# Row sums of a banded softmax: one reduction on VectorE in place of eight accumulators on ScalarE, with the units of all engines in a new order

## The reference

```python
def local_attention(q, k, v):
    b, h, n, d = q.shape
    w = n // WINDOW
    bq = q.reshape(b, h, w, WINDOW, d) * QK_SCALE
    ...
    sim = jnp.einsum('bhwid,bhwjd->bhwij', bq, bk)
    ...
    mask = (i < j) | (i > j + WINDOW) | (j == -1)
    sim = jnp.where(mask, -jnp.finfo(sim.dtype).max, sim)
    attn = jax.nn.softmax(sim, axis=-1)
    out = jnp.einsum('bhwij,bhwjd->bhwid', attn, bv)
```

## Time and profile before

| | |
|---|---|
| median of 3 runs | 1740.66 us (1738.55 to 1747.6) |
| profiled execution | 1741.72 us, its span 1739.9 us |
| granted TensorE clock, mean | 0.924 of full speed |
| PE busy | 1434.9 us, 82% |
| VectorE (DVE) busy | 1254.2 us, 72%, 2201 instructions |
| ScalarE (ACT) busy | 1268.0 us, 73%, 2878 instructions |
| GpSimd (POOL) busy | 367.3 us, 21% |

### The profile page before, as it was taken

How to read it: one execution, slowest core, us unless ns; L and a number is a source line. 1 busy time by engine, 2 the same in 40 slices (tenths; PEclk the granted TensorE clock), 3 DMA queues, 4 the chain that set the end, 5 groups by cost and what they waited for, 6 DMA issues and landing times.

```text
span 1739.9 us, 32913 instructions
## 1 busy us (share of the span) xinstructions
PE 1434.9 (82%) x13044; PEld 849.7 (49%) x13044; DVE 1254.2 (72%) x2201; ACT 1268.0 (73%) x2878; POOL 367.3 (21%) x222
## 2 busy tenths in 40 slices
PE   3667697889888998888889887789798898988986
PEld 1122454345556554445456534555345564656664
DVE  6999978565886549968786878764977685477554
ACT  5523792779668787787798484878588985898875
POOL 2000000003144130410252021221003451045440
PEclk8776996899999999899999998989899998999998
DMA  7774224013023012323003433003320140000100
GB/s 250 232 242 138 73 76 98 3 26 74 11 52 60 23 39 84 117 81 121 19 19 81 92 105 103 16 9 88 106 98 17 24 94 10 10 17 20 31 20 19
DMA packets 70985, 121.75 MB, mean 70 GB/s; under 512 B 6864, under 2 KB 28112, under 8 KB 69072
## 3 DMA queue, kind: packets, MB, share of 16 engines
q1 hardware_dynamic: 70832, 119.65, 24.5%
HBM read 89.34 MB, written 15.60 MB: 60 GB/s over the span
## 4 chain that ended last, share of the span: by engine, by line
PE 36%; ACT 28%; DVE 28%; issue 5%; DMA 1%; POOL 0%; SPq 0%; ACTq 0%; DVEq 0%; POOLq 0%
ACT tiles L1591 8%; ACT L1425 5%; PE psum L602 5%; DVE neg_max L1197 5%; DVE tiles L1119 5%; PE psum L848 4%; DVE tiles L1113 2%; DVE tiles L1123 2%; PE psum L880 2%; ACT tiles L1535 2%; ACT tiles L1632 2%; PE psum L881 2%; PE psum L833 2%; PE psum L980 2%; PE psum L947 2%
## 5 line engine op out<-in xcount | busy, mean ns | idle before, releaser
L1754 POOL TENSOR_TENSOR tiles<-tiles 128x1024 f32<-128x1024 f32 x64 | 155.1, 2424 | 669.7 <-DVE tiles L1376 669.7
L602 PE MATMUL psum<-cst,tiles 128*128 128x128 f32 x1408 | 211.4, 287 | 87.9 <-DVE tiles L1337 32.6
L602 PEld LDWEIGHTS psum<-cst,tiles 128*128 128x128 f32 x1408 | 163.3, 146 | 164.9 <-issue 102.5
L1591 ACT ACTIVATE tiles<-psum,lmax,invn 128x128 f32<-128x128 f32 x512 | 226.3, 470 | 15.2 <-DVE lmax L1247 11.8
L1197 DVE TENSOR_REDUCE neg_max<-psum 128x2 f32<-128x1024 f32 (+3 forms) x176 | 189.8, 1117 | 32.5 <-PE psum L800 32.3
L673 PE MATMUL psum<-tiles,cst 128*128 128x512 f32 x256 | 152.4, 728 | 43.1 <-DVE tiles L1123 43.1
L1765 POOL TENSOR_TENSOR tiles<-tiles,lsum 128x1024 f32<-128x1024 f32 x64 | 126.9, 1983 | 280.7 <-DVE lsum L1251 280.7
L1425 ACT ACT_TABLE_LOAD x124 | 159.1, 1283 | 2.9 <-PEq L1968 0.7
L1119 DVE TENSOR_TENSOR_SCAN tiles<-tiles 128x512 f32<-128x512 f32 x128 | 157.2, 1259 | 2.7 <-ACT tiles L1484 0.5
L1484 ACT ACTIVATE tiles<-tiles,colp 128x512 f32<-128x512 f32 x128 | 90.3, 719 | 87.3 <-DVE tiles L1119 79.1
L1232 DVE TENSOR_REDUCE ssq<-tiles 128x16 f32<-128x1024 f32 x64 | 77.8, 1215 | 86.3 <-ACT tiles L1680 86.0
(11 more groups left out here) (226 smaller groups left out, 3324.4 us busy)
## 6 DMA issues: line engine op xcount, KB each, us to landing
tiles<-bc_scratch SPq DMA_DIRECT2D x128, 512.0 KB, 4.8
v_prev<-tiles SPq DMA_DIRECT2D x112, 128.0 KB, 2.3
split_scratch<-tiles SPq DMA_DIRECT2D x96, 128.0 KB, 2.4
tiles<-split_scratch SPq DMA_DIRECT2D x32, 384.0 KB
wts<-in_wts SPq DMA_DIRECT2D x1, 3114.0 KB, 15.8
tiles<-in_x SPq DMA_DIRECT2D x8, 256.0 KB, 3.8
out<-tiles SPq DMA_DIRECT2D x8, 256.0 KB, 2.7
tiles<-in_rowp SPq DMA_DIRECT2D x1, 768.0 KB, 7.4
```

What stands on the lines that cost most here:

```text
L602: ins = nc.tensor.transpose(ps[:, j * 128:(j + 1) * 128], src[:, j * 128:(j + 1) * 128], ident)
L1591: ins = fn(pr[:, i * 128:(i + 1) * 128], ps[:, i * 128:(i + 1) * 128], ACT.Exp, bias=own(lmax)[:, b, i:i + 1], scale=own(invn)[:, j, 0, 2 ...
L1754: tt(T(TURNED, 2), T(TURNED, 2), T(TURNED + 2, 2), ALU.add).then_inc(sem("qk_sum"), 1)
```

## The change

Three edits. l_exp no longer accumulates. l_inv first reduces the 128x1024 probabilities in SBUF to eight sums, waits for its own reduction, and takes the reciprocal. ORDER and BANKS are replaced as a whole, for all engines; network(), the units and their number stay (1570 units on PE, 1226 on VectorE, 1394 on ScalarE, 202 on GpSimd, 204 on SyncE), and the order now gives 125 table loads where it gave 124.

```diff
 def l_inv(l, j):
     dve.wait_ge(*at("l_exp", l, j))
+    step(nc.vector.tensor_reduce(own(lsum)[:, j % 2, :], T(LP, 2).rearrange("p (i n) -> p i n", n=128), AX.X, ALU.add))
+    settle()
     nc.vector.reciprocal(own(lsum)[:, j % 2, :], own(lsum)[:, j % 2, :]).then_inc(sem("l_inv"), 1)
...
             ins = fn(pr[:, i * 128:(i + 1) * 128], ps[:, i * 128:(i + 1) * 128], ACT.Exp,
-                     bias=own(lmax)[:, b, i:i + 1], scale=own(invn)[:, j, 0, 2 * g + e:2 * g + e + 1],
-                     accum_out=own(lsum)[:, b, i:i + 1])
+                     bias=own(lmax)[:, b, i:i + 1], scale=own(invn)[:, j, 0, 2 * g + e:2 * g + e + 1])
...
 ORDER = {
     "PE": (
...
-        "65745f65865b65c65d65e65965a65f"),
+        "55e75855f75b75c75975a75d75e75f"),
...
 BANKS = (
...
-    "65432502456704676574570656746204654545432043257270717257041040650431240135243767567675767657657657")
+    "02140767276535675657430274645606756724570454564230103743737603450765076767760760667607107176076010")
```

More of the change, by code:

```diff
@@ L312 @@
[L312 to L318 removed]
+        "80010000010110200100210300380130030130210420030310520120200420300510610700600730430510820410900800920530630710a20610c10b"
@@ new lines @@
+        "00a10f10e10d00c10g00b00f00e00d20710h00g10i30810j00h00i30900j10k20810l10n10p10m10o10q30a10r00k00l00n00p00m00o00q30c00r10s"
+        "30b10t10u10v10w20920a30f30e30d20c00s30g00t00u00v00w20b30h10y10x10z11011111211b11g11e11c11d11i11f11h11711911811411511311a"
+        "11600y00x00z01101001230i01b20f01g01e20e01d01c11j01f20d01i01h01711l11k11n01411m11o11q11p11s11r11w11t11v01830j11x11z12111u"
+        "11y12312012212412612712512901901a12812a12c12e12b12d12f12h12i12g12k01512j12l12n12p30k12m12o01312q01620g12r30l12s30n12t30p"
@@ new lines @@
+        "01j30m30o30q20h30r01l01k01n20i01m01o01q01s01p01r01w01v12u01t20j12v01x01z02101u01y12w02002202302613502402702502902802a02c"
+        "12x02e12y02b02d13402f02h02i30s02g02k02j02l02n30t02m02o02p12z13613702q13d02r30v02s30u30w02t13013120k13813213f13e13g13320l"
+        "13m20n20p13a13913h20m20o20q13b13n13o20r13p13c13j13i13q13k02u13l02v02w03513s13r30y30x13t13u30z13v02x31002y20s13w03402z20t"
+        "13x20v20u20w31114214313y13z14014103603714403003114503d14614714g03803203e03331214814914f14a03f03g03m03a03903h31b03b14h03n"
@@ new lines @@
+    "POOL": (
+        "80180010000010110230010410510310710810610a10b10910c00100220000400500310d10e00700800610g10h10f00a00b00910j10k10i00c10m10n"
+        "10l10o00d00e00g00h00f00j00k00i00m00n00l00o30130230430530330730830620120230a30b30920420520330c20720820650020a20b20920c30d"
+        "30e30g30h30f30j30k20d30i20e30m30n40020g20h30l20f20j30o20k20i20m20n20l20o401700402600501502404405403504505503407408406506"
+        "50750840a40b60160250a40950b50960460560360760860660a60b60960c40c50c60d60e60g60h60f70170260j60k60i60m60n70460l70570340d40e"
+        "60o70770870640g40h70a70b70970c50d50e40f40j40k50g50h40i40m40n50f50j50k40l50i50m50n40o70d70e50l70g70h70f50o70j70k70i70m70n"
+        "70l70o"),
@@ new lines @@
+    "SP": (
+        "10000080480180680780880080280580380980a20080b101001300102103002003104301105201004005302303106202107006007203304305108204"
+        "10900800920530630720620730830920820910a10b10c00a00b00c10d10e00d00e10f10g30a10h30b10i30c00f00g20a20b20c10j00h10k00i10l10m"
+        "00j00k10n50000l50150200m30d30e50350450550650750850900n40040140220d20e40330f40430g40540640740840930h20f20g30i20h50a50b20i"
+        "50c30j30k20j20k30l40a30m40b40c20l20m30n70040d40e70170270370470570660020n70770850d60170950e60260360460560660760860940f40g"
+        "50f50g70a60a60b70b60c70c60d60e40h40i50h60f60g70d50i70e60h60i60j60k70f70g60l60m70h70i60n40j50j40k50k40l70j40m70k50l50m70l"
+        "70m40n50n70n"),
@@ L329 @@
[L329 to L332 removed]
+    "012101020000101212122340454510440440001104514411041041041415210024202104206420606060604620420420640235635057075305305702"
@@ new lines @@
+    "020467026400274062035032507024602476737654320203573046046702357373573203042600462343642040160304505125732374134735430714"
+    "071761767107603507074201750232430735425432012302562201673621025632525670574347347067264701037037124012612045473052747041"
+    "021010102463452061430670670602460246767027474626076476076276742066230401035701351312354560264060240260126012402352426045"
+    "020254046760245057607607013570724624062013503753576030303013535315771103103405703707765065346350107106352510526250302757"
@@ new lines @@
+    "275602230430163063713453676576121017236706706727072374262345640676547306757270467272045654540254676204016701201401410612"
+    "106454067010707637012013213176315713757175610567560246042604624620461024101624124661235765071357035270030403570333573757"
+    "010350335035373732560262440024022012461246176513750130404667776654364657547357076542701107451470230402604502345654204424"
+    "024024040240240240240101023042620624072042670461313513070135713513075026464360254560524646204460267674623232402606070240"
```

226 lines of the change are left out of this document (98 added, 128 removed).

## The result

The changed kernel takes 1712.99 us (median of 4 runs, 1710.49 to 1715.73) against 1743.43 us (4 runs of before on the same chip, 1738.55 to 1747.6): ratio 0.9825, 95% interval 0.9801 to 0.9849. That is 1.75% less, 30 us, where 15 us had been forecast; it lies in the range that was given. The experiments will show that the 15 us were put together from terms of which hardly one holds.

What follows compares the result with a forecast made beforehand. VectorE led the first four batches' state scans, TensorE everything behind, no engine full. Terms -30 (ScalarE) + 14 (VectorE) + 1 (table load) = -15 us gave 1726 us; its own range 1712 to 1733, whole range 1696 to 1764.

Steps and rivals of the forecast that it cites:

- ScalarE's 30 us: Banded softmax exponentials without accumulators: 0.74 us less per unit, 47 us of ScalarE's time, 30 us of it on the chain.
- the PSUM row: Trace row of normalization L1632 reading PSUM without accumulator, 0.343 us each, taken as the new exponential's duration.
- all do: Upper bound on ScalarE's saving: all 64 exponential units matter on the chain, 47 us.
- VectorE's 14 us: Added row-sum reductions: 80 us of VectorE's time, 29 on the chain at weight 0.36, half charged; bounds 0 and 29.
- The new order at nothing: The replaced order on all engines: no term of its own in the sum; spread scans said to help a little.
- rival (c): The new order by itself is much better, recovering a tenth of TensorE's idle time: 20 us more, 1706 us; chance 0.08.
- Rival (a): A wash: VectorE takes over ScalarE's gain, 1741 us, or the exponential saves only the SBUF row's amount, 1740; chance 0.24.
- rival (b): Slower: VectorE becomes late, its reductions holding other batches' work; +13 (1754 us) to +27 (1768), middle 1761; chance 0.28.
- One more table load, +1: ScalarE's table loads, 125 instead of 124: 0.7 us more on the chain, counted as 1.
- SyncE's queue, nothing: SyncE's re-sorted queue with the same transfers: priced at nothing, DMA having 1% of the chain; bound 19 us.
- The signs I had named: Profile signs of a right forecast: operation durations, busy times, exponentials' chain share down a fifth, row-sum wait at most 45 us.

Runs made afterwards that it cites:

- experiment 6: The changed kernel with a second, equal row-sum reduction behind the first in each of its 64 units: 1763.16 us, ratio 1.0105.

## Why the prediction was right in its range and wrong in its steps

**ScalarE's 30 us.** Right locally: 0.74 us a unit, from the PSUM row. The estimate by the Trainium skill's page "ScalarE: Activation LUTs", section "What ACT_TABLE_LOAD costs", would have given less; with 0.343 us an exponential the trace goes against it for PSUM. Wrong on the chain. In the order of before the accumulators cost 14 or 20 us, not 30. I multiplied the operation's share of the chain by how much shorter it got; but chain time that is taken away goes to whoever was next, and the share fell from 141 to 33 us for a saving of 47. In the new order the same removal gives 54 to 58 us, outside my bound of 47 ("all do").

**VectorE's 14 us.** The 78 us, 1219 ns each, are right. Its busy time came to 1313 us and not 1334, since L1113 and the scans got shorter under the new order and L1316 with either part, a gain that no term had. The weight was not. I computed 29 and then charged half, because I expected the order to give the sums good places. In the old order they cost 22 and 28, so the 29 was near the right term for the exchange alone; in the new order they cost 10 and 6, less than the 14 charged.

**The new order at nothing.** This is the step that failed most. With the reduction in place the order is worth -37 us, and with accumulators +19. I had it in rival (c) at 0.08 and looked for a merit of its own, spread scans; the rows show none that holds for all units. Its merit is conditional: it is there for exponentials without accumulators (-37 and -25) and gone with them (+19 and -3). That the old order was fitted to its own units in the same way is my reading of the table; my forecast of the exchange charged nothing for breaking such a fit. Rival (a)'s sum for the exchange, -30 + 29, would have said a wash; it is +9, which is rival (b) in that order near its low value of +13 (VectorE's chain share 34%, VectorE late in 47 units). That the total fell in the range is therefore luck, two errors that half cancel: exchange -15 forecast, +9 measured; order 0 forecast, -37 or so measured. If the half that I took off the sums' cost is booked to the order, as my reason for it was, the pairs are -1 and +9, -14 and -37, and the step fails all the same.

**One more table load, +1.** 125 loads are there, and yet their chain time fell from 92 to 50 us. Counting loads was the wrong view; it matters where they stand. But their leaving the chain does not by itself make the kernel faster: they have 2.9 to 3.7% in all four kernels of the new order and 5.1 to 5.3% in all four of the old one, and the order's effect goes from +19 to -37 us. What part of the 37 us the loads' places have, and what part the fit to the new units or the banks, stays open.

**SyncE's queue, nothing.** No row speaks against it: DMA has 2% of the chain after, 1% before.

**Rivals.** (a) is near the exchange without a new order, if one takes +9 for a wash. (b) tells its mechanism, as far as the chain and the 47 late units show it, and in experiment 6 the cost beyond the planned 80 us has a weight of 50/80 = 0.63. (c) had the right part and too small a size; the measured 1713 lies nearer to its 1706 than to the 1726 of the forecast. The signs I had named: exponentials 2.74, reductions 78 us in all, ScalarE near 1223 (1229) came, the last one 6 us off; the exponential's share down by a fifth and the wait at or under 45 us did not, though the time fell twice as far as forecast. Both signs stood for the old order with the cheaper unit, and that kernel showed them (1.9% and 19.8 us) and was slower.

## What to carry to other kernels

Where every engine runs a written order, a unit's duration and the order are one thing. Price a change of durations at the old order from measured weights, expect it to lose the fit (here +9 us for an exchange that frees ScalarE, -37 for planning again), and do not judge an order with units other than those it was made for. Do not take an operation's share of the chain times its saving as the gain, nor a wait of an in-order engine as a fault: the changed kernel waits more at the row sum than the one before. The dose run (the cost left out, once, twice) costs little and tells how much room an order has.

## What the runs showed of the hardware

The granted clock differs from schedule to schedule, so a delay may cost more than itself. Whole span and mean granted clock of the changed kernel, of the new order with the old units, and of the old order with the sum earlier:

```profile
core 0: 1714.0 us, clock 0.931
```

```profile
core 0: 1759.1 us, clock 0.922
```

```profile
core 0: 1802.8 us, clock 0.911
```

The time at 1.2 GHz, 2 x (1 - clock) x span, is 237, 274 and 321 us (before: 264). Much of the first difference lies in one stretch. From 1200 to 1500 us, the changed kernel and then the new order with the old units (busy us, granted clock):

```profile
1200.00:1500.00 300.00, 258.01 (x2847) 160.07 (x2846) 209.78 (x353) 213.61 (x428) 91.86 (x56) 0.94 0.17 37
```

```profile
1200.00:1500.00 300.00, 251.91 (x2601) 151.14 (x2602) 178.23 (x350) 215.37 (x520) 76.07 (x47) 0.90 0.16 35
```

TensorE did 246 matmuls fewer there, in 6 us less of busy time. A busy microsecond at the lower level loses about half a microsecond of work, so 37 us more of it are worth up to 19 us; this may be why 47 us of ScalarE cost 58 and 54. That 19 us is an upper bound. A lower figure comes from one and the same kernel: the 39 executions of the kernel before whose clock is on record have 0.919 (1750.66 us) to 0.932 (1738.77 and 1740.86 us), and a straight line through them gives 7 us less for each 0.01 more. By it the 0.009 between the two kernels is worth 6 us and not 19, and the 0.007 between before and after 5 us. Both are arguments from the records, since no run changed the clock by itself, and there is no general law here: with the reduction made twice the clock was 0.929 and the kernel still 50 us longer.

The accumulator read shows 219 ns but lengthens an exponential by 92 only (0.435 against 0.343 us from start to start). And the VectorE operations with two inputs in SBUF named above (L1113, L1247, L1316) take longer beside GpSimd's work, while the reductions, with one, do not: in the changed kernel 17 of the 64 small products of L1247 overlap an operation of GpSimd and take 987 ns on average, the 47 others 167; of the reductions of L1251, 32 overlap one and take 1216 ns on average, the others 1218.
